# Where the rotary tables of a two-layer AdaLN network are formed, and which engine issues a transformer's first loads

## The reference, cut to what matters

```python
def attn_layer(x, Wqkv, qs, ksc, Wo):
    q, k, v = jnp.split(x @ Wqkv, 3, -1)          # 16 heads of 64, 256 tokens
    q = l2norm(q) * qs                            # qs, ksc: 64 factors per layer
    k = l2norm(k) * ksc
    freqs, scale = rotary_tables(n)
    cos, sin = (jnp.cos(freqs), jnp.sin(freqs))
    q = q * cos * scale + rotate_half(q) * sin * scale
    k = k * cos * (1 / scale) + rotate_half(k) * sin * (1 / scale)
    return local_attention(q, k, v) @ Wo
for i in range(6):
    x = attn_layer(shift_tokens(x), ...) + x
    x = ffn_layer(shift_tokens(x), ...) + x
```

## Time and profile before

| | us |
|---|---|
| median of 3 runs | 4747.47 (4742.75 to 4749.88) |
| the profiled execution, its own time | 4748.92 |
| its span, first to last instruction | 4747.2 |
| mean granted clock of PE | 0.963 of full speed |
| PE, DVE, ACT, POOL busy | 4319.4, 3144.3, 2720.9, 2628.5 |
| opening block | 0 to about 197.5 |
| transformer block | 199 to about 3565 |

### The profile page before, as it was taken

The page is one execution under the profiler, slowest core; times in us unless marked ns, Lnnn a source line. Parts: engine busy times, 40 slices in busy tenths (PEclk is TensorE's granted clock), DMA queues, the critical chain, the costliest instruction groups (busy, mean ns, idle before and its releaser), DMA issues. The chain is left out here.

```text
span 4747.2 us, 156031 instructions
## 1 busy us (share of the span) xinstructions
PE 4319.4 (91%) x69192; PEld 2792.5 (59%) x69192; DVE 3144.3 (66%) x4110; ACT 2720.9 (57%) x3930; POOL 2628.5 (55%) x1468
## 2 busy tenths in 40 slices
PE   7489999999999999999999999999975999788868
PEld 5256666666666666666666666666652554344435
DVE  4477776777667776777767777777733443699974
ACT  4246666666666666666656666666642443577743
POOL 0266666666666666666666666666622112477752
PEclk8699999999999999999999999999986999899999
DMA  2111212221222112211122122211111000211110
GB/s 56 52 34 42 48 45 64 49 48 45 54 54 52 44 46 59 56 44 45 44 62 50 44 49 58 55 44 47 46 30 33 1 1 1 93 72 72 72 35 16
DMA packets 230431, 221.12 MB, mean 47 GB/s; under 512 B 137657, under 2 KB 185794, under 8 KB 227714
## 3 DMA queue, kind: packets, MB, share of 16 engines
q1 hardware_dynamic: 229761, 211.13, 17.0%
HBM read 68.50 MB, written 4.03 MB: 15 GB/s over the span
## 5 line engine op out<-in xcount | busy, mean ns | idle before, releaser
L1018 POOL TENSOR_TENSOR tf_qk<-tf_qk,tf_rot 128x1024 f32<-128x1024 f32 x384 | 909.7, 2369 | 1135.0 <-DVE tf_rot L1396 1134.3
L1084 PE MATMUL tf_psum<-tf_Wqkv,tf_xsT 128*128 128x512 f32 x1536 | 738.3, 603 | 45.3 <-issue 20.0
L1025 POOL TENSOR_TENSOR tf_qk<-tf_qk,tf_rn 128x1024 f32<-128x1024 f32 x384 | 722.6, 1903 | 63.4 <-ACT tf_rn L1277 63.4
L1270 ACT ACTIVATE tf_sq<-tf_psum 128x1024 f32<-128x1024 f32 x384 | 393.9, 1026 | 507.9 <-DVE tf_rot L1396 507.9
L1392 DVE TENSOR_TENSOR tf_qk<-tf_psum,tf_table 128x1024 f32<-128x1024 f32 x384 | 467.6, 1218 | 239.3 <-PE tf_psum L1084 235.7
L1402 DVE TENSOR_REDUCE tf_ss<-tf_sq 128x16 f32<-128x1024 f32 x384 | 457.8, 1192 | 23.4 <-ACT tf_sq L1270 23.4
L1396 DVE TENSOR_TENSOR tf_rot<-tf_psum,tf_table 128x1024 f32<-128x1024 f32 x384 | 466.4, 1215 | 0.0
L1084 PEld LDWEIGHTS tf_psum<-tf_Wqkv,tf_xsT 128*128 128x128 f32 x1536 | 271.4, 192 | 325.2 <-issue 299.3
L1066 PE MATMUL tf_psum<-ident,tf_qk 128*128 128x128 f32 x3072 | 405.5, 275 | 22.1 <-ACT tf_qT L1292 2.4
L1150 PE MATMUL tf_psum<-tf_probT,tf_Vback 64*64 64x32 f32 x12288 | 396.1, 222 | 26.6 <-DVE tf_z L1437 16.0
L1066 PEld LDWEIGHTS tf_psum<-ident,tf_qk 128*128 128x128 f32 x3072 | 344.0, 141 | 112.8 <-issue 110.6
(11 more groups left out here) (319 smaller groups left out, 7961.8 us busy)
## 6 DMA issues: line engine op xcount, KB each, us to landing
tf_Vback<-tf_V SPq DMA_DIRECT2D x384, 128.0 KB
tf_Vback<-tf_V SPq DMA_DIRECT2D x576, 64.0 KB
mb_Csb<-mb_kept SPq DMA_DIRECT2D x16, 2048.0 KB, 7.1
tf_zr<-z SPq DMA_DIRECT2D x96, 128.0 KB, 2.7
z<-tf_z SPq DMA_DIRECT2D x48, 256.0 KB, 2.5
tf_Wqkv<-in_Wqkv_split SPq DMA_DIRECT2D x18, 512.0 KB, 3.8
tf_zu<-z SPq DMA_DIRECT2D x97, 64.0 KB
tf_zu<-z SPq DMA_DIRECT2D x97, 63.5 KB
```

The source lines that it names most:

```text
L1018: nc.gpsimd.tensor_tensor(v, v, rot[:, kind, :], ALU.add).then_inc(added.sem, 1)
L1025: nc.gpsimd.tensor_tensor(v, v, rn[:, t, HEADS * kind:HEADS * (kind + 1)].unsqueeze(2) .to_broadcast([P, HEADS, HD]), ALU.mult).then_inc(n ...
L1084: last = nc.tensor.matmul(proj[:, half, :], xsT[:, step.unit(0), WIN + t * P:WIN + (t + 1) * P], Wqkv[:, c:c + 512], start=True, stop=True)
L1270: nc.scalar.activation(sq[:, kind, :], flat2(proj), ACT.Square).then_inc(squared.sem, 1)
```

## The change

The six rotary products move from DVE in the transformer block to POOL in the opening block. The base, the six factors and the first four results lie in `z`, the last two in `Wcg`. POOL waits for the base and factors (`rope_in`) and for the last write of the polar part (`q_stored`), forms the tables, and forms `Wcg` only after the tables have landed in DRAM (`tables_saved`). SP issues the loads and the saves at the end of its stream of the opening block. ACT waits for `tables_saved` before it writes `z`.

In the transformer block, ACT issues layer 0's q columns, both halves of its table, and its k columns, ahead of everything else it does. SP issues the mask, waits for `zeroed` at 3 instead of 6, and issues the first input, the v columns, the residuals, the output weights and the feed-forward's loads. Each group of loads has a semaphore of its own: SP waits for `first_q`, counts `q_ok` up, waits for `first_k`, and so on, and then goes on to `load_input(1)`. The tiles `tf_base` and `tf_hold` are gone. One semaphore of a later stage (`ah_loaded`) and the DRAM tensor of the tables are taken at the start of the program.

```diff
@@ opening_stage @@
+        places = z[:, :, :].rearrange("p n c -> p (n c)")
+        base = places[:, 0:512].rearrange("p (s t e) -> p s t e", s=4, t=TT)
+        mult = places[:, 512:2048].rearrange("p (l s e) -> p l s e", l=DEPTH, s=4)
+        table_place = lambda l: (places[:, 2048 + l * 512:2560 + l * 512] if l < 4 else
+                                 Wcg[:, :, :].rearrange("p b c -> p (b c)")[:, (l - 4) * 512:(l - 3) * 512])
...
                 sp.dma_start(dst[:, :, :], kept[:, m, part, :].unsqueeze(0).to_broadcast([P, B, P])).then_inc(rows_in, 16)
+            sp.dma_start(base, d["rope"]).then_inc(rope_in, 16)
+            for l in range(DEPTH):
+                sp.dma_start(mult[:, l, :, :], d["rope_scales"][l:l + 1, :, :].to_broadcast([P, 4, HD])).then_inc(rope_in, 16)
+            for l in range(DEPTH):
+                sp.wait_ge(tabled, l + 1)
+                sp.dma_start(k.tables[l], table_place(l).rearrange("p (s t e) -> p s t e", s=4, t=TT)).then_inc(tables_saved, 16)
+            sp.wait_ge(tables_saved, 16 * DEPTH)
...
         def _(pool):
+            pool.wait_ge(rope_in, 16 + 16 * DEPTH)
+            pool.wait_ge(q_stored, B + 1)
+            for l in range(DEPTH):
+                nc.gpsimd.tensor_tensor(table_place(l).rearrange("p (s t e) -> p s t e", s=4, t=TT), base,
+                                        mult[:, l, :, :].unsqueeze(2).to_broadcast([P, 4, TT, HD]), ALU.mult)\
+                    .then_inc(tabled, 1)
             pool.wait_ge(rows_in, 48)
             pool.wait_ge(w_in, 64)
+            pool.wait_ge(tables_saved, 16 * DEPTH)
...
             inverse_rms(NP - 1)
+            act.wait_ge(tables_saved, 16 * DEPTH)
@@ transformer_stage, SP @@
-            sp.dma_start(base[:, :, :, :], d["rope"]).then_inc(consts, 16)
             sp.dma_start(mask32[:, :, :], d["local_mask"]).then_inc(consts, 16)
-            for l in range(DEPTH):
-                sp.dma_start(mult[:, l, :, :], d["rope_scales"][l:l + 1, :, :].to_broadcast([P, 4, HD])).then_inc(mults, 16)
...
-            sp.wait_ge(zeroed, 6)
+            sp.wait_ge(zeroed, 3)
             load_input(0)
+            load_columns(0, 2, first_v)
             load_residual(0, 0)
             load_residual(1, 1)
-            for kind in range(3):
-                load_columns(0, kind)
-            load_out_weights(0)
-            load_ff_weights(0)
-            for l in range(DEPTH):
-                sp.wait_ge(tabled, l + 1)
...
-                sp.dma_start(tables[l], flat[:, l % 4 * 512:(l % 4 + 1) * 512].rearrange("p (s t e) -> p s t e", s=4, t=TT))\
-                    .then_inc(tables_saved, 16)
-            sp.wait_ge(tables_saved, 16 * DEPTH)
-            load_table(0, 0)
-            load_table(0, 1)
-            loads = 10
-            sp.wait_ge(weights, 16 * loads)
-            for e in (q_ok, k_ok, v_ok, out_ok, ff_ok):
-                sp.sem_inc(e.sem, 1)
+            load_out_weights(0, first_out)
+            load_ff_weights(0, first_ff)
+            loads = 0
+            for landed, count, ok in ((first_q, 3, q_ok), (first_k, 1, k_ok), (first_v, 1, v_ok), (first_out, 1, out_ok),
+                                      (first_ff, 4, ff_ok)):
+                sp.wait_ge(landed, 16 * count)
+                sp.sem_inc(ok.sem, 1)
             sp.wait_ge(filled, 1)
             load_input(1)
@@ transformer_stage, ACT @@
+            act.dma_start(Wqkv[:, 0:INNER], d["Wqkv_split"][0, :, 0:INNER]).then_inc(first_q, 16)
+            for t in range(TT):
+                act.dma_start(table[:, :, t, :], k.tables[0, :, :, t, :]).then_inc(first_q, 16)
+            act.dma_start(Wqkv[:, INNER:2 * INNER], d["Wqkv_split"][0, :, INNER:2 * INNER]).then_inc(first_k, 16)
             act.sem_inc(copied, 1)
             act.wait_ge(zeroed, 6)
@@ transformer_stage, DVE @@
-            dve.wait_ge(consts, 32)
+            dve.wait_ge(consts, 16)
...
-            dve.wait_ge(mults, 16 * DEPTH)
-            for l in range(DEPTH):
-                target = (hold if l < 4 else prob)[:, :, :, :, :].rearrange("p t a b e -> p (t a b e)")
```

More of the change, by code:

```diff
@@ L787, in transformer_stage @@
         eps = sb("eps", [P, 1])
-        base = sb("base", [P, 4, TT, HD])
         table = sb("table", [P, 4, TT, HD])
@@ L808, in transformer_stage @@
         oT = sb("oT", [P, TT, PAIRS, P])
-        hold = sb("hold", [P, TT, PAIRS, 2, HD])
         mx = sb("mx", [P, TT, 2, PAIRS])
@@ L824, in transformer_stage @@
         hT = sb("hT", [P, 3, 4 * P])
-        tables = nc.dram_tensor("tf_tables", (DEPTH, P, 4, TT, HD), F32, kind="Internal").ap()
-        mult = probT[:, :, :, :].rearrange("p t a c -> p (t a c)")[:, 0:DEPTH * 4 * HD]\
-            .rearrange("p (l s e) -> p l s e", l=DEPTH, s=4)
         psum = k.ps(ctx, "tf_psum", [P, 8, 512])
@@ L834, in transformer_stage @@
         ev = lambda name, n=1: Event(nc, ctx, "tf_" + name, n)
-        consts, mults, zeroed, masks_ready, tabled, tables_saved, weights = sems(
-            nc, ctx, "tf_consts tf_mults tf_zeroed tf_masks_ready tf_tabled tf_tables_saved tf_weights")
+        consts, zeroed, masks_ready, weights, first_q, first_k, first_v, first_out, first_ff = sems(
+            nc, ctx, "tf_consts tf_zeroed tf_masks_ready tf_weights tf_first_q tf_first_k tf_first_v tf_first_out tf_first_ff")
         filled, copied = sems(nc, ctx, "tf_filled tf_copied")
@@ L855, in _, with load_columns, load_table, load_out_weights @@
                 e.start(sp)
-            sp.dma_start(base[:, :, :, :], d["rope"]).then_inc(consts, 16)
             sp.dma_start(mask32[:, :, :], d["local_mask"]).then_inc(consts, 16)
-            for l in range(DEPTH):
-                sp.dma_start(mult[:, l, :, :], d["rope_scales"][l:l + 1, :, :].to_broadcast([P, 4, HD])).then_inc(mults, 16)
-            def load_columns(l, kind):
+            def load_columns(l, kind, landed=weights):
                 sp.dma_start(Wqkv[:, kind * INNER:(kind + 1) * INNER],
[L863 to L875, removed]
+                             d["Wqkv_split"][l, :, kind * INNER:(kind + 1) * INNER]).then_inc(landed, 16)
+            def load_table(l, t, landed=weights):
+                sp.dma_start(table[:, :, t, :], k.tables[l, :, :, t, :]).then_inc(landed, 16)
+            def load_out_weights(l, landed=weights):
+                sp.dma_start(Wo[:, :, :], d["L0_ffn_Wo"][l].rearrange("(c p) n -> p c n", p=P)).then_inc(landed, 16)
+            def load_ff_weights(l, landed=weights):
+                sp.dma_start(W1[:, :], d["L0_ffn_W1"][l]).then_inc(landed, 16)
+                sp.dma_start(W2[:, :, :], d["W2_b2"][l].rearrange("(c p) n -> p c n", p=P)).then_inc(landed, 16)
+                sp.dma_start(b1[:, :], d["ff_b1"][l]).then_inc(landed, 16)
+                sp.dma_start(ln_gb[:, :], d["ln_gb"][:, l, :]).then_inc(landed, 16)
             def load_input(u):
@@ L1377, in _ @@
             nc.vector.memset(ss[:, :, :, 1:2], 1e-24).then_inc(masks_ready, 1)
-            dve.wait_ge(mults, 16 * DEPTH)
-            for l in range(DEPTH):
-                target = (hold if l < 4 else prob)[:, :, :, :, :].rearrange("p t a b e -> p (t a b e)")
-                nc.vector.tensor_tensor(target[:, l % 4 * 512:(l % 4 + 1) * 512].rearrange("p (s t e) -> p s t e", s=4, t=TT),
-                                        base[:, :, :, :], mult[:, l, :, :].unsqueeze(2).to_broadcast([P, 4, TT, HD]),
-                                        ALU.mult).then_inc(tabled, 1)
             def rope(step, kind):
@@ L2289, in __init__ @@
         self.rows = [k.sb(ctx, "ah_rows", [P, B // 2, 3, P])]
-        self.loaded, = sems(k.nc, ctx, "ah_loaded")
+        self.loaded = k.ahead_loaded
     def vectors(self, half):
@@ L2713, in build @@
         k.vectors = nc.dram_tensor("vectors", [B, 4, 3, P], F32, kind="Internal").ap()
+        k.ahead_loaded, = sems(nc, ctx, "ah_loaded")
+        k.tables = nc.dram_tensor("tables", [DEPTH, P, 4, TT, HD], F32, kind="Internal").ap()
         with ExitStack() as first:
```

6 lines of the change are left out of this document (2 added, 4 removed).

## The result

Over 20 runs of each kernel the median went from 4745.88 us (4735.74 to 4763.66) to 4733.53 us (4725.50 to 4746.78). The ratio is 0.9971, with a 95% interval of 0.9962 to 0.9979: 13.8 us less by the ratio, between 10 and 18, and 12.4 by the medians.

A forecast was written before the change was run, and what follows sets the result against it. SP's chain of issues and table transfers was taken to bound the transformer's start; 3.24 + 1.04 + 13.0 = 17.28 us saved, giving a span of 4729.9 and a median of 4730.2 us, range 4726 to 4735.

The forecast's parts named there:

- What bounds the kernel, and what moves the end: Transformer start, 210 to 227 us: compute engines wait for SP's chain; a start earlier by x moves the end by x.
- First piece: SP's issues ahead of the first input, transformer start: only the mask is left of 3.72 us, saving 3.24 us.
- Second piece: SP's issues from first input to last feed-forward load: two column issues go to ACT, 10.64 us become 9.60, saving 1.04.
- Third piece: Table saves and reads before the first projection, 13.10 us: a wait and count of 0.1 us remain, 13.0 us go.
- What may be late next: Transformer start: input copy done by 207.9 (slack 1.7 us), first_q landed by 208.6, second input with 16 us of slack.
- The opening: Opening block: POOL forms tables from 68.7 to 76.3 us, op_Wcg by 88.8, 69 us of slack, no cost to the scan.
- Rival B: Opening block: POOL's products hold up the scan's DVE product by 6.6 us, giving 4736.8 us; chance 0.04.
- The clock: PE's clock in the transformer: same pattern of levels, moved up with the work; 3.6 us either way if the rise shifts.
- D: Pipeline's start in the transformer: PE's clock stays low, 1.79 us more per projection, ten steps give 4766 us; chance 0.03.
- Rival A: Transformer start: ACT's transfers and the input share DMA engines, input 4.8 us late, gain 14.2 us, 4733.3 us; chance 0.12.
- a sign of A: Transformer start: a first projection at 212 us or later, released by ACT's copy, would show that the loads meet.
- the sign that I named for a wrong sum: Transformer start: an ACT issue far above 0.6 us would make the summed gain of 17.28 us wrong.

## Why the prediction was right, and where its size was off

**What bounds the kernel, and what moves the end.** Right, as far as it can be measured. The stretch in which nothing computes shrank from 27 to 14 us. The stage lost 13.9 us, and the whole time fell by 13.8 with an interval of 10 to 18, which can't confirm that the end moved one to one.

**First piece, issues ahead of the input (3.24 us).** Measured 203.16 less 199.44 before and 200.65 less 200.26 after: 3.33 us. But those microseconds were not worth as much on the path: with ACT's transfers under way, an input that went out 1.16 us later ended its third piece at the same time.

**Second piece, SP's issues (9.60 us).** This is the term that was mis-sized: it took 12.96 us (200.65 to 213.61), 3.36 more; the third piece of the input alone took 3.43 more. I had taken SP's issue times over from before as if they belonged to the instructions. They depend on what is under way: the same row took 2.74, 3.35, 4.77 and 6.25 us with 0, 0.25, 1 and 1.25 MB on ACT's queue. The trace of before had the sign as well: in the opening, three broadcast rows of one shape (`L275`), issued one behind the other, took 0.38, 3.01 and 5.27 us.

**Third piece, the table's way (13.0 us).** Right: 0.17 us are left between the end of SP's last issue and the projection, 0.1 taken. But it is not the tables' move alone that gives them. SP now waits for each group of loads by its own semaphore; behind its last issue it waited 2.1 us more for the output weights and 1.8 for `ln_gb`, and came to `load_input(1)` at 217.91. With one wait for all loads, as before, the first projection would have come there, some 4 us later. That is an estimate from this trace; no run takes the split out.

**What may be late next.** Right in kind. ACT's issues took 0.42, 1.29 and 0.71 us, 2.4 in all for the 2.3 taken. The input's copy ended at 211.91, 1.9 us ahead of the projection, for a slack of 1.7 foreseen. Counted from SP's first issue, the copy was 3.2 us and the projection 3.3 us later than foreseen. `load_input(1)` was issued at 217.91 and nothing waited for it: PE turned the second input at 244.23, released by ACT.

**The opening.** Right: the tables from 70.5 to 77.9 (68.7 to 76.3 foreseen), `op_Wcg` by 85.0, 73 us ahead of its first use, no scan product of DVE longer than before. Rival B is out.

**The clock.** Right: same pattern, moved up with the work, but for the short rise at 217. D did not happen.

**Rival A**, the loads meet, is in kind what the kernel did, and its 14.2 us was closer than the forecast's 17.3. That its number fits is in part luck: I had it act by the input's landing, 4.8 us late and released by ACT's copy, and set it aside because the last piece went out behind ACT's last transfer. The input was late, 8.5 us from the start of the third piece's issue to PE where it had been 5.2, yet it was not last: the projection at 213.78, beyond the 212 named as a sign of A, was released by SP. What I did not ask is what else ACT's transfers do: they held up SP's issue. And the sign that I named for a wrong sum, a long issue on ACT, was looked for on the wrong engine: ACT's longest row was 0.71 us. Of the issue time that ACT takes off SP nothing was left: 13.29 us without ACT, 13.04 and 13.52 with it. By the rule of the Trainium skill weighed in the prediction (DMA: Bandwidth & Descriptors, "Issuing engines are not separate DMA queues"), transfers interleave on the same 16 DMA engines whoever issues them, and a second issuing engine saves issue time alone. The runs agree that the transfers meet, 2.74 us for the third piece alone and 6.25 beside ACT's, and show nothing left of the issue time.

## What to carry to other kernels

When a start-up chain of loads is costed, the time of an issue is not a property of its row: ask what is under way when it comes, and which row follows a transfer that leaves one partition out. Moving work off the start-up chain (here the tables, 13 us) was worth what the timeline said, with the wait for the other loads split off too; moving issues to a second engine may only move the wait. For a change of a few microseconds in a kernel of 4.7 ms, a stage between two places of the trace, which repeated within 0.5 us, tells more than 20 whole times do.

## What the runs showed of the hardware that I had not expected

The same instructions did not take the same time from run to run, stage by stage. The opening took 196.5 to 201.9 us in the twelve traces that have the changed opening, the transformer from its first projection 3317.6 to 3335.2 us over all fourteen, and the last block took either about 181.4 or about 183.8 us, in kernels whose instructions there are the same but for the first loads. No experiment was made on this, and its cause stays open. It is why the two spans differ by 16.0 us where the edited stage differs by 13.9, and why single times of these kernels say little.
